# Output projection of the mixing stage as three products of high and low parts, W_out gated and split in pieces

## The chip, the core and the metric

One core of one Trainium2 chip runs the whole program. The metric is the device time of that core in microseconds, from the first to the last instruction with the launch's own overhead around it; the median of three runs counts.

## The reference

The block takes x (4 batches of 1024 tokens, 256 wide) and six modulation rows per batch, of which `ga` gates the mixing branch.

```
h = layernorm(x) * (1 + ca) + sa
xn = rms_scale * h / (norm(h) + 1e-8) * split_scale
K = sigmoid(xn @ W_K);  u, g_in, g_out = split(xn @ W_ugg, 3)
u = u * sigmoid(g_in) * (1 - K)
outputs = scan over time of (Kshift, u)
x = x + ga * (outputs * sigmoid(g_out) @ W_out + h)
h = layernorm(x) * (1 + cb) + sb
x = x + gb * mixture_of_experts(h)        # top 2 of 8, gelu, 256 -> 1024 -> 256
```

All of it is float32. What the change touches is the product `outputs * sigmoid(g_out) @ W_out`, with `ga` already multiplied into the columns of W_out.

## The kernel before

The program has two stages. The mixing stage (0 to about 287 us) handles 4096 tokens in 8 groups of 512 (`NG`), two groups to a batch; the expert stage, which this change leaves alone, handles sorted tiles of 256 tokens. Every engine has its program written out by hand, in order; semaphores connect them, and each engine runs strictly in its own order.

In a group g the hidden width of 512 is cut in four parts hc of 128. Where full precision is wanted, a float32 operand is rounded to a high part in a faster format (fp32r), the low part is what the rounding left out, and a product is taken as high*high + high*low + low*high. The kernel before does that for the main products, not for the output projection.

TensorE, `main(g, hc)`: 24 products of 512 columns into the four banks mm[0] to mm[3] (K, g_in, u, g_out), in two halves `main_part`. `project(g, hc)`, L814: four float32 products of 256 columns, `og` with `wog`, each recorded as two passes. Between them the turns `turn_xn` (L804) and `turn_h2` (L832), `logits` and `rank`. The order in a group is main_part(0), turn_h2(g-2), main_part, project(g-1, 3), logits(g-2), main(g,1), project(g,0), rank(g-2), main(g,2), project(g,1), main_part(g,3,0), turn_xn(g+1), main_part(g,3,1), project(g,2).

ScalarE, `gates_in` and `gate_out`: the sigmoids of K into `kb` (L643), of g_in into `sgi` (L646), of g_out in place (L651). Between them the scalings and squares of the two norms (`sqj`, `sqk`, L612, L621, L628, L659, L668), the high part `xh` of the turned input (L635), the copies of turned h2 (L675) and the gate sigmoid `sgw` (L680).

VectorE, `recur(g, hc)`: four steps of 128x512, L1046 (u times g_in, releases `u_gated`), L1049, the scan L1052 and the output gate `og` (L1057), double-buffered; for even g a copy of the scan's last column, `cy`. Between the four calls stand the small chains of the norms (`ln1_stats`, `ln1_norm`, `ln2_stats`), the choice of experts (`top2`, `place`, `gate_weights`), `xn_low` (L1039) and `add_y` (L1070, L1075), which takes the finished projection out of PSUM. A function `weave` issues one step of each of several chains in turn, since each step of a chain waits for the one before it.

GpSimd: `ln1_modulate`, `ln2_modulate` and `gate_h`, two 128x1024 operations each (L471 and L474, L497 and L500, L490 and L491), paced by `u_gated` through `beside`; `gate_wout(b)` (L480), one operation of 128x1024 per batch that makes `wog`, double-buffered; and `send`, four indirect DMA issues at a time (L510) that put rows of h2 in their experts' lists.

Around the change the order of GpSimd and ScalarE counts most. GpSimd's loop before:

```
for g in range(NG):
    if g == 0:
        gate_wout(0)
        ln1_modulate(1)
    beside(g, 0)
    gate_h(g)
...
    if g % 2 == 1 and g + 1 < NG:
        gate_wout(g // 2 + 1)
...
    if g >= 2:
        send(g - 2, 0)
```

## Time and profile before

| | |
|---|---|
| median of 3 runs | 784.33 us (784.13 to 784.36) |
| the profiled execution | 783.47 us, its span 781.5 us |
| mean granted TensorE clock | 0.956 |
| TensorE busy | 707.0 us, 90% of the span |
| VectorE busy | 534.0 us, 68% |
| ScalarE busy | 421.0 us, 54% |
| GpSimd busy | 399.8 us, 51% |
| chain that ended last | TensorE 70%, VectorE 12%, issue 8% |
| of it the output projection, L814 | 6% |

PE stands for TensorE's products, PEld for its weight loads, DVE for VectorE, ACT for ScalarE, POOL for GpSimd. Busy time is the time in which an engine has at least one operation under way; an operation that stands still on the engine counts as busy. The mixing stage is the first 287 of the 781.5 us.

### The profile page before, as it was taken

The page shows a single profiled execution, that of the slowest core. Times are in us where ns is not written, and L with a number is a line of the kernel's source. Part 1 is how long each engine was busy: PE and PEld are TensorE (multiplying, and loading weights), DVE is VectorE, ACT ScalarE, POOL GpSimd, SP SyncE. Part 2 cuts the span into 40 slices and gives each one's busy share as a digit, 9 for nine tenths or more (in the row PEclk, how much of TensorE's full clock was granted, in tenths as well). Part 3 has the DMA queues.
Part 4 walks back from the last instruction along what each step waited for, and adds up shares of the span by engine and source line. Part 5 has one row for each costly group of instructions (what it writes and reads, how often), then busy time and mean ns, then how long its engine had stood idle before and what let it go on. Part 6 is the DMA issues. An engine that isn't in the chain of part 4 may idle for free.

```text
span 781.5 us, 17355 instructions
## 1 busy us (share of the span) xinstructions
PE 707.0 (90%) x4854; PEld 652.7 (84%) x4854; DVE 534.0 (68%) x1787; ACT 421.0 (54%) x1082; POOL 399.8 (51%) x309
## 2 busy tenths in 40 slices
PE   4899999999999964699998999989889989999992
PEld 1778888888888853699998999989879989989991
DVE  6878879989796768375557655576684576485551
ACT  6466555655545342356656556656446565565560
POOL 1355647777583465445436435454554363463443
PEclk9899999999999995699999999999898999999997
DMA  8531012130120522534364343747423644433432
GB/s 298 163 137 55 3 54 97 54 110 29 55 76 22 177 83 77 184 57 68 65 145 96 63 75 62 175 110 179 109 46 61 138 105 109 81 54 66 68 70 41
DMA packets 50309, 72.56 MB, mean 93 GB/s; under 512 B 5808, under 2 KB 42108, under 8 KB 50240
## 3 DMA queue, kind: packets, MB, share of 16 engines
q0 software_dynamic: 16480, 27.28, 19.3%
q1 hardware_dynamic: 33760, 44.46, 18.1%
q8 instruction: 30, 0.49, 0.3%
q14 instruction: 39, 0.32, 0.1%
HBM read 48.85 MB, written 22.87 MB: 92 GB/s over the span
## 4 chain that ended last, share of the span: by engine, by line
PE 70%; DVE 12%; issue 8%; ACT 3%; DMA 3%; another core or an unknown queue 1%; POOL 1%; DVEq 0%; POOLq 0%; ACTq 0%
PE mm L945 21%; PE mm L789 19%; PE yb L955 18%; PE yb L814 6%; PE tp L924 2%; DMA out_x<-ysb,tokb 1%; DVE hl L1307 1%; DVE SL L238 1%; PE tp L845 1%; DMA gbr<-mod_rows,xm 1%; PE tp L804 1%; PE tp L832 1%; DVE fl L1271 1%; DVE SH L230 1%
## 5 line engine op out<-in xcount | busy, mean ns | idle before, releaser
L763 ACT ACTIVATE h<-mm,b1T 128x256 f32<-128x256 f32 (+1 forms) x288 | 134.4, 467 | 187.9 <-PE mm L945 116.0
L1307 DVE TENSOR_TENSOR hl<-h,hh 128x256 fp32r<-128x256 f32 (+1 forms) x288 | 121.0, 424 | 139.7 <-ACT hh L764 107.5
L555 POOL DMA_INDIRECT out_x<-ysb,tokb x68 | 112.5, 1654 | 202.2 <-DVE ysb L1338 170.3
L945 PE MATMUL mm<-fh,SH 128*128 128x256 f32 x576 | 166.3, 289 | 21.0 <-DVE fl L1271 13.8
L955 PE MATMUL yb<-SH,hh 128*128 128x256 f32 x544 | 157.9, 290 | 9.7 <-DVE hl L1307 9.4
L945 PE MATMUL mm<-fl,SH 128*128 128x256 f32 x576 | 164.8, 286 | 0.0
L945 PE MATMUL mm<-fh,SL 128*128 128x256 f32 x576 | 164.5, 286 | 0.0
L955 PE MATMUL yb<-SH,hl 128*128 128x256 f32 x544 | 153.6, 282 | 0.0
L955 PE MATMUL yb<-SL,hh 128*128 128x256 f32 x544 | 153.3, 282 | 0.0
L764 ACT ACTIVATE hh<-mm,b1T 128x256 fp32r<-128x256 f32 (+1 forms) x288 | 133.7, 464 | 0.0
L945 PEld LDWEIGHTS mm<-fh,SH 128*128 128x128 f32 x576 | 112.6, 195 | 23.6 <-issue 23.6
L955 PEld LDWEIGHTS yb<-SH,hh 128*128 128x128 f32 x544 | 103.2, 190 | 12.2 <-DVE hl L1307 11.1
L945 PEld LDWEIGHTS mm<-fl,SH 128*128 128x128 f32 x576 | 112.3, 195 | 0.0
L945 PEld LDWEIGHTS mm<-fh,SL 128*128 128x128 f32 x576 | 112.3, 195 | 0.0
L789 PE MATMUL mm<-xh,WH 128*128 128x512 f32 x256 | 107.0, 418 | 1.5 <-DVE xl L1039 1.4
L955 PEld LDWEIGHTS yb<-SL,hh 128*128 128x128 f32 x544 | 103.4, 190 | 0.0
L955 PEld LDWEIGHTS yb<-SH,hl 128*128 128x128 f32 x544 | 103.2, 190 | 0.0
L789 PE MATMUL mm<-xh,WL 128*128 128x512 f32 x256 | 101.2, 395 | 0.0
L789 PE MATMUL mm<-xl,WH 128*128 128x512 f32 x256 | 100.5, 393 | 0.0
L550 POOL DMA_INDIRECT gbr<-mod_rows,xm x74 | 75.7, 1022 | 22.6 <-issue 22.6
L510 POOL DMA_INDIRECT disp_x<-h2all,pos x64 | 63.6, 994 | 28.9 <-issue 26.2
L814 PE MATMUL yb<-wog,og 128*128 128x256 f32 x256 | 60.3, 379 | 0.0
(217 smaller groups left out, 1182.7 us busy)
## 6 DMA issues: line engine op xcount, KB each, us to landing
...
gbr<-mod_rows,xm POOLq DMA_INDIRECT x74
```

What stands on the lines that cost most here:

```text
L230: e.tensor_copy(SH[n % 2][:, r], wraw[n % 2][:, r]).then_inc(done, 1)
L510: e.indirect_dma_start(out=Xd, out_offset=bass.IndirectOffsetOnAxis(ap=p[:, j:j + 1], axis=0), in_=h2all[:, j, :], in_offset=None).then_in ...
L550: e.indirect_dma_start(out=gbr[:, j, :], out_offset=None, in_=modd.rearrange("b (n d) -> (b n) d", d=D), in_offset=bass.IndirectOffsetOnAx ...
L555: e.indirect_dma_start(out=out_rows, out_offset=bass.IndirectOffsetOnAxis(ap=tokb[:, j:j + 1], axis=0), in_=ysb[:, j, :], in_offset=None, ...
L763: e.activation(h32[:, f % 2, c_], mm[f % 4][:, c_], ACT.Gelu_apprx_tanh, bias=bias)
L764: e.activation(hh[:, f, c_], mm[f % 4][:, c_], ACT.Gelu_apprx_tanh, bias=bias)\
L789: i = e.matmul(mm[q][:, :], a[:, k, c0:c0 + 128], b[:, g % 2, k, :], start=(k == 0 and t == 0), stop=(k == 1 and t == 2))
L814: i = e.matmul(yb[j // 2][:, (j % 2) * D:(j % 2 + 1) * D], og[:, n % 2, j * 128:(j + 1) * 128], wog[:, (g // 2) % 2, hc, :], start=(hc == ...
L924: i = e.transpose(tp[k][:, j * 128:(j + 1) * 128], xin[:, j, k * 128:(k + 1) * 128], ident[:, :])
L945: i = e.matmul(mm[f % 4][:, 0:TE], a[:, k, f * 128:(f + 1) * 128], b[:, k, :], start=(k == 0 and t == 0), stop=(k == 1 and t == 2))
L955: i = e.matmul(yb[0][:, j * D:(j + 1) * D], a[:, f, j * 128:(j + 1) * 128], b[:, f, :], start=(f == 0 and j == 0 and t == 0), stop=(f == N ...
L1307: e.tensor_tensor(hl[:, f, w_], h32[:, f % 2, w_], hh[:, f, w_].bitcast(F32), ALU.subtract)\
```

## The change

Each call of `project` takes three fp32r products for every float32 product before: `oh` with `wgh`, `oh` with `wgl`, `ol` with `wgh`. For that, `og` (now one buffer) is copied by ScalarE to its high part `oh` (`o_high`), and VectorE subtracts (`o_low`) to get `ol`; `project` waits for `o_low`. `o_high(n-1)` stands in `gates_in` of the next part, between `kb` and `sgi`. `o_low` stands alone after `add_y` (hc 0) and after `recur(g, 2)`, and is woven into the chains that follow for hc 1 (after four steps) and hc 3 (after three).

W_out times `ga` is made in four pieces of 128x256 per batch. GpSimd multiplies a piece into `wgt` (two buffers, `gate_wout(b, h)`), ScalarE copies it to `wgh` (`wout_high`), GpSimd subtracts it to `wgl` (`wout_low`). `wgh` and `wgl` have one buffer, so a piece of the next batch waits for the last `project` that reads it. The pieces are issued at the start of the first group of a batch, ahead of `gate_h`, not at the end of the group before it. For the first batch `modulate(1)` on VectorE replaces `ln1_modulate(1)` on GpSimd. To make room, `sqk` is gone (its operation shares `sqj`), and two small buffers of the start lie in others.

The core of the diff (the new semaphores `wout_high`, `wout_low`, `o_high`, `o_low` and the small buffers are left out):

```diff
...
             ob = sb(p1, "ob", [128, T])
-            og = sb(p1, "og", [128, 2, T])
-            wog = sb(p1, "wog", [128, 2, 4, D])
+            og = sb(p1, "og", [128, T])
+            oh = sb(p1, "oh", [128, 2, T], F32R)
+            ol = sb(p1, "ol", [128, 2, T], F32R)
+            wgh = sb(p1, "wgh", [128, 4, D], F32R)
+            wgl = sb(p1, "wgl", [128, 4, D], F32R)
+            wgt = sb(p1, "wgt", [128, 2, D])
...
             sqj = sb(p1, "sqj", [128, 4, D])
-            sqk = sb(p1, "sqk", [128, 4, D])
...
-            def gate_wout(b):
+            def gate_wout(b, h):
...
                 e.wait_ge(S[f"mod_loaded{b % 3}"], 16 * (b // 3 + 1))
-                past(e, "projected", 8 * (b - 1))
-                e.tensor_tensor(wog[:, b % 2, :, :], wo[:, :, :], bc(mod(b, 2), 4), ALU.mult)\
-                    .then_inc(S["wout_gated"], 1)
+                past(e, "wout_low", 4 * b + h - 1)
+                e.tensor_tensor(wgt[:, h % 2, :], wo[:, h, :], mod(b, 2), ALU.mult).then_inc(S["wout_gated"], 1)
+            def wout_low(b, h):
+                e.wait_ge(S["wout_high"], 4 * b + h + 1)
+                e.tensor_tensor(wgl[:, h, :], wgt[:, h % 2, :], wgh[:, h, :].bitcast(F32), ALU.subtract)\
+                    .then_inc(S["wout_low"], 1)
...
             for g in range(NG):
-                if g == 0:
-                    gate_wout(0)
-                    ln1_modulate(1)
+                if g % 2 == 0:
+                    gate_wout(g // 2, 0)
+                    gate_wout(g // 2, 1)
+                    wout_low(g // 2, 0)
+                    gate_wout(g // 2, 2)
+                    wout_low(g // 2, 1)
+                    if g == 0:
+                        gate_wout(0, 3)
+                    wout_low(g // 2, 2)
+                    if g == 0:
+                        wout_low(0, 3)
...
                 gate_h(g)
+                if g and g % 2 == 0:
+                    gate_wout(g // 2, 3)
...
                     ln1_modulate(g + 2)
+                if g and g % 2 == 0:
+                    wout_low(g // 2, 3)
...
                     ln2_modulate(g - 1)
-                if g % 2 == 1 and g + 1 < NG:
-                    gate_wout(g // 2 + 1)
...
                 past(e, "h_squared", g)
+                past(e, "x2_squared", g - 2)
...
                     e.activation(xh[:, g % 2, k, :], tp[k][:, :], ACT.Copy).then_inc(S["xn_high"], 1)
+            def wout_high(b, h):
+                e.wait_ge(S["wout_gated"], 4 * b + h + 1)
+                past(e, "projected", 4 * (2 * b - 1) + h + 1)
+                e.activation(wgh[:, h, :], wgt[:, h % 2, :], ACT.Copy).then_inc(S["wout_high"], 1)
+            def o_high(n):
+                e.wait_ge(S["o_gated"], n + 1)
+                past(e, "projected", n - 1)
+                e.activation(oh[:, n % 2, :], og[:, :], ACT.Copy).then_inc(S["o_high"], 1)
...
                 e.activation(kb[:, hc, 1:T + 1], mm[0][:, :], ACT.Sigmoid).then_inc(S["k_ready"], 1)
+                if n:
+                    o_high(n - 1)
...
                 past(e, "x2_squared", g)
+                e.wait_ge(S["h_squared"], min(g + 3, NG))
                 for j in range(4):
-                    i = e.activation(sqk[:, j, :], x2b[:, g % 2, j, :], ACT.Square, bias=sm2[:, 1, j:j + 1],
+                    i = e.activation(sqj[:, j, :], x2b[:, g % 2, j, :], ACT.Square, bias=sm2[:, 1, j:j + 1],
...
             for g in range(NG):
+                if g and g % 2 == 0:
+                    for h in range(3):
+                        wout_high(g // 2, h)
...
                 gate_out(g, 0)
+                if g and g % 2 == 0:
+                    wout_high(g // 2, 3)
...
                 gates_in(g, 1)
+                if g == 0:
+                    for h in range(4):
+                        wout_high(0, h)
...
             g = NG - 1
+            o_high(4 * NG - 1)
...
                 n = 4 * g + hc
-                e.wait_ge(S["o_gated"], n + 1)
-                e.wait_ge(S["wout_gated"], g // 2 + 1)
+                e.wait_ge(S["o_low"], n + 1)
+                e.wait_ge(S["wout_low"], 4 * (g // 2) + hc + 1)
...
                 for j in range(4):
-                    i = e.matmul(yb[j // 2][:, (j % 2) * D:(j % 2 + 1) * D], og[:, n % 2, j * 128:(j + 1) * 128],
-                                 wog[:, (g // 2) % 2, hc, :], start=(hc == 0 and j % 2 == 0), stop=(hc == 3),
-                                 skip_group_check=True)
+                    for t, (a, b) in enumerate(((oh, wgh), (oh, wgl), (ol, wgh))):
+                        i = e.matmul(yb[j // 2][:, (j % 2) * D:(j % 2 + 1) * D], a[:, n % 2, j * 128:(j + 1) * 128],
+                                     b[:, hc, :], start=(hc == 0 and j % 2 == 0 and t == 0), stop=(hc == 3 and t == 2),
+                                     skip_group_check=True)
...
+            def modulate(g):
+                e.wait_ge(S["x_scaled"], g + 1)
+                link(e, e.tensor_tensor(hb[:, g, :, :], hb[:, g, :, :], bc(mod(0, 1), 4), ALU.mult), "dve_a")
+                e.tensor_tensor(hb[:, g, :, :], hb[:, g, :, :], bc(mod(0, 0), 4), ALU.add).then_inc(S["h_ready"], 1)
...
                 e.wait_ge(S["out_gated"], n + 1)
-                past(e, "projected", n - 1)
-                e.tensor_tensor(og[:, n % 2, :], ob[:, :], mm[3][:, :], ALU.mult).then_inc(S["o_gated"], 1)
+                past(e, "o_high", n)
+                past(e, "o_low", n)
+                e.tensor_tensor(og[:, :], ob[:, :], mm[3][:, :], ALU.mult).then_inc(S["o_gated"], 1)
...
                     link(e, e.tensor_copy(cy[:, hc:hc + 1], ob[:, T - 1:T]), "dve_a")
+            def o_low(n, rounds):
+                for _ in range(rounds):
+                    yield
+                e.wait_ge(S["o_high"], n + 1)
+                past(e, "projected", n - 1)
+                e.tensor_tensor(ol[:, n % 2, :], og[:, :], oh[:, n % 2, :].bitcast(F32), ALU.subtract)\
+                    .then_inc(S["o_low"], 1)
...
             e.wait_ge(S["mod0_copied"], 2)
-            e.wait_ge(S["x_scaled"], 1)
-            link(e, e.tensor_tensor(hb[:, 0, :, :], hb[:, 0, :, :], bc(mod(0, 1), 4), ALU.mult), "dve_a")
-            e.tensor_tensor(hb[:, 0, :, :], hb[:, 0, :, :], bc(mod(0, 0), 4), ALU.add).then_inc(S["h_ready"], 1)
+            modulate(0)
...
             for g in range(NG):
+                n = 4 * g
+                low = [o_low(n - 1, 3)] if g >= 1 else []
...
                 elif g + 2 < NG:
-                    weave(ln1_stats(g + 2), ln1_norm(g + 1))
+                    weave(ln1_stats(g + 2), ln1_norm(g + 1), *low)
                 elif g + 1 < NG:
-                    weave(ln1_norm(g + 1))
+                    weave(ln1_norm(g + 1), *low)
+                else:
+                    weave(*low)
...
                     add_y(g - 1)
+                else:
+                    modulate(1)
+                weave(o_low(n, 0))
...
                 if g == 0:
-                    weave(ln1_norm(1), ln1_stats(2))
-                weave(*([ln2_stats(g - 1)] if g >= 1 else []), *([place(g - 2), gate_weights(g - 2)] if g >= 2 else []))
+                    weave(ln1_norm(1), ln1_stats(2), o_low(n + 1, 4))
+                else:
+                    weave(ln2_stats(g - 1), *([place(g - 2), gate_weights(g - 2)] if g >= 2 else []), o_low(n + 1, 4))
...
                 recur(g, 2)
+                weave(o_low(n + 2, 0))
...
                 recur(g, 3)
+            weave(o_low(4 * NG - 1, 0))
...
```

The order on GpSimd from the end of group 3 to the start of group 4. In it `disp_x<-h2all` is `send`, `wog` and `wgt` are W_out times `ga`, `wgl` its low part. Before:

```order
L497 TENSOR_TENSOR h2all<-h2all,mb 128x4x256 [waits s_x2_scaled]
L500 TENSOR_TENSOR h2all<-h2all,mb 128x4x256 [waits s_u_gated,s_pool_own]
L480 TENSOR_TENSOR wog<-wo,mb 128x1024 [waits s_projected,s_mod_loaded2,s_wout_loaded]
L510 DMA disp_x<-h2all,pos 34816x264 [waits s_pads_sent0,s_pads_zeroed,s_weights_ready,s_places_ready]
L510 DMA disp_x<-h2all,pos 34816x264 x3
```

With the change:

```order
L507 TENSOR_TENSOR h2all<-h2all,mb 128x4x256 [waits s_u_gated,s_pool_own]
L517 DMA disp_x<-h2all,pos 34816x264 [waits s_pads_sent0,s_pads_zeroed,s_weights_ready,s_places_ready]
L517 DMA disp_x<-h2all,pos 34816x264 x3
L483 TENSOR_TENSOR wgt<-wo,mb 128x256 [waits s_wout_low,s_mod_loaded2,s_wout_loaded] x2
L487 TENSOR_TENSOR wgl<-wgt,wgh 128x256 [waits s_wout_high]
L483 TENSOR_TENSOR wgt<-wo,mb 128x256 [waits s_wout_low,s_mod_loaded2,s_wout_loaded]
L487 TENSOR_TENSOR wgl<-wgt,wgh 128x256 [waits s_wout_high] x2
L497 TENSOR_TENSOR hb<-hb,mb 128x1024 [waits s_xn_ready,s_x_loaded1,s_mod_loaded2,s_u_gated]
```

The operation on W_out stood ahead of the sends; its pieces now stand behind them.

The order on ScalarE at the same place, from the squares that end group 3 (`sqj`) to the sigmoids of part 0 of group 4. Before:

```order
L621 ACTIVATE sqj,ss<-hb 128x256 x3
L641 ACTIVATE kb<-zcol 128x1 [waits s_k_ready,s_scanned]
L643 ACTIVATE kb<-mm 128x512 [waits s_main_done,s_act_own]
L646 ACTIVATE sgi<-mm 128x512 [waits s_u_gated,s_main_done]
L675 ACTIVATE h2T<-tp 128x512 [waits s_h2_turned,s_logits_done]
```

With the change:

```order
L640 ACTIVATE sqj,ss<-hb 128x256 x3
L659 ACTIVATE wgh<-wgt 128x256 [waits s_projected,s_wout_gated] x3
L670 ACTIVATE kb<-zcol 128x1 [waits s_k_ready,s_scanned]
L672 ACTIVATE kb<-mm 128x512 [waits s_main_done,s_act_own]
L664 ACTIVATE oh<-og 128x512 [waits s_projected,s_o_gated]
L677 ACTIVATE sgi<-mm 128x512 [waits s_u_gated,s_main_done]
L707 ACTIVATE h2T<-tp 128x512 [waits s_h2_turned,s_logits_done]
```

Three copies `wgh` now stand ahead of `kb`, and wait for GpSimd (`wout_gated`); `oh` stands between `kb` and `sgi`.

The order on VectorE at `recur(3, 2)` and behind it. Before:

```order
L1046 TENSOR_TENSOR mm<-mm,sgi 128x512 [waits s_main_done,s_in_gated]
L1049 SCALAR_TENSOR_TENSOR mm<-kb,mm 128x512 [waits s_u_gated,s_k_ready]
L1052 SCALAR_TENSOR_TENSOR ob<-kb,cy,mm 128x512 [waits s_w_ready]
L1057 TENSOR_TENSOR og<-ob,mm 128x512 [waits s_projected,s_out_gated,s_scanned]
L1039 TENSOR_TENSOR xl<-tp,xh 128x512 [waits s_xn_high] x2
L1046 TENSOR_TENSOR mm<-mm,sgi 128x512 [waits s_main_done,s_in_gated]
```

With the change:

```order
L1093 TENSOR_TENSOR mm<-mm,sgi 128x512 [waits s_main_done,s_in_gated]
L1096 SCALAR_TENSOR_TENSOR mm<-kb,mm 128x512 [waits s_u_gated,s_k_ready]
L1099 SCALAR_TENSOR_TENSOR ob<-kb,cy,mm 128x512 [waits s_w_ready]
L1105 TENSOR_TENSOR og<-ob,mm 128x512 [waits s_o_high,s_o_low,s_out_gated,s_scanned]
L1115 TENSOR_TENSOR ol<-og,oh 128x512 [waits s_projected,s_o_high]
L1086 TENSOR_TENSOR xl<-tp,xh 128x512 [waits s_xn_high] x2
L1093 TENSOR_TENSOR mm<-mm,sgi 128x512 [waits s_main_done,s_in_gated]
```

`ol` stands between the output gate and `xl`, and waits for ScalarE's `o_high`.

## Rows read from the trace of the kernel before

**Rows 1.** windows, columns us, then busy (x) of PE, PEld, DVE, ACT, POOL

```profile
134.40:167.14 32.74, 32.23 (x163) 26.86 (x162) 30.79 (x115) 18.01 (x48) 25.74 (x17) 1.00 0.23 76
```

**Rows 2.** chain that ended last: start us, us, what

```profile
167.14 1.73 PE yb L814 x8
168.98 5.61 PE mm L789 x24
...
344.50 1.42 PE yb L955 x12
```

**Rows 3.** waits of DVE, 134.4 to 167.1 us: total, times, longest

```profile
DVE xl L1039 <- ACT xh L635: 0.4, 1, 0.4
```

**Rows 4.** timeline of DVE: start us, us, engine line op

```profile
110.61 0.70 DVE L1046 TENSOR_TENSOR mm<-mm,sgi 128x512 f32<-128x512 f32 x1
...
131.37 2.16 DVE L1104 TENSOR_TENSOR rt<-Lg,mx 128x32 f32<-128x32 f32 x1
...
143.85 0.70 DVE L1046 TENSOR_TENSOR mm<-mm,sgi 128x512 f32<-128x512 f32 x1
...
148.99 0.69 DVE L1046 TENSOR_TENSOR mm<-mm,sgi 128x512 f32<-128x512 f32 x1
...
151.83 0.69 DVE L1057 TENSOR_TENSOR og<-ob,mm 128x512 f32<-128x512 f32 x1
152.43 1.40 DVE L989 BATCH_NORM_STATS2 bst<-xb 128x6 f32<-128x256 f32 x4
153.75 0.84 DVE L1008 TENSOR_SCALAR nt<-ss 128x4 f32<-128x4 f32 x1
...
157.72 0.68 DVE L1046 TENSOR_TENSOR mm<-mm,sgi 128x512 f32<-128x512 f32 x1
...
162.77 1.68 DVE L1075 TENSOR_SCALAR sm<-sm 128x4 f32<-128x4 f32 x1
...
167.38 0.69 DVE L1046 TENSOR_TENSOR mm<-mm,sgi 128x512 f32<-128x512 f32 x1
...
172.71 0.18 DVE L1126 TENSOR_SCALAR exw<-sgw 128x36 f32<-128x36 f32 x1 [0.72 <-ACT sgw L680]
...
175.64 0.70 DVE L1046 TENSOR_TENSOR mm<-mm,sgi 128x512 f32<-128x512 f32 x1
...
241.09 0.70 DVE L1046 TENSOR_TENSOR mm<-mm,sgi 128x512 f32<-128x512 f32 x1
```

**Rows 5.** timeline of ACT

```profile
147.14 1.10 ACT L635 ACTIVATE xh<-tp 128x512 fp32r<-128x512 f32 x2
...
150.52 0.41 ACT L621 ACTIVATE sqj<-hb 128x256 f32<-128x256 f32 x1
...
153.20 0.60 ACT L643 ACTIVATE kb<-mm 128x512 f32<-128x512 f32 x1 [0.89 <-PE mm L789]
...
171.47 0.60 ACT L643 ACTIVATE kb<-mm 128x512 f32<-128x512 f32 x1
```

**Rows 6.** timeline of POOL

```profile
147.05 2.43 POOL L497 TENSOR_TENSOR h2all<-h2all,mb 128x1024 f32<-128x1024 f32 x1
149.82 2.37 POOL L500 TENSOR_TENSOR h2all<-h2all,mb 128x1024 f32<-128x1024 f32 x1 [0.34 <-DVE mm L1046]
...
154.71 0.99 POOL L510 DMA_INDIRECT disp_x<-h2all,pos  x1 [0.15 <-issue]
...
159.55 2.38 POOL L490 TENSOR_TENSOR hb<-hb,mb 128x1024 f32<-128x1024 f32 x1
```

**Rows 7.** line L238, duration ns min/median/max

```profile
L238 DVE TENSOR_TENSOR SL<-h2all,SH x20: 678/684/5294, 328.3 to 693.8; 128x512 fp32r<-128x512 f32 x20
```

**Rows 8.** timeline of PE, idle before in brackets

```profile
49.44 1.10 PE L804 MATMUL tp<-ident,xnb 128*128 128x128 f32 x8 [1.37 <-ACT xnb L628]
```

**Rows 9.** PE at 553.5, and the window behind it (PEclk after the engines)

```profile
553.50 0.58 PE L955 MATMUL yb<-SH,hh 128*128 128x256 f32 x1 [3.69 <-DVE hl L1307]
...
553.40:560.00 6.60, 6.50 (x32) 6.50 (x33) 4.20 (x13) 2.44 (x6) 1.87 (x2) 0.54 0.55 173
```

More of the change, by code:

```diff
@@ L35 @@
     "c_silu", "scale_made", "mod_made", "mod0_copied", "mod_copied", "mod_guarded", "mod_written", "mod_loaded0",
-    "mod_loaded1", "mod_loaded2", "zero_made", "pads_zeroed", "w_high", "w_low", "wout_gated", "b1_copied",
+    "mod_loaded1", "mod_loaded2", "zero_made", "pads_zeroed", "w_high", "w_low", "wout_gated", "wout_high", "wout_low", "o_high", "o_low", "b1_copied",
     "x_stats", "x_scaled", "h_ready", "h_squared", "rms_ready", "xn_ready", "xn_turned", "xn_high", "xn_low",
@@ L71, in build @@
         zcol = sb(ctx, "zcol", [128, 1])
-        vrow = sb(ctx, "vrow", [76, 128])
         vT = sb(ctx, "vT", [128, 76])
@@ L78, in build @@
         bgb = sb(ctx, "bgb", [128, E])
-        ioi = sb(ctx, "ioi", [128, 210], I32)
         iof = sb(ctx, "iof", [128, 210])
@@ L163, in build @@
         modr = x2f[0:NB, 0:6 * D]
+        ioi = x2f[:, 0:210].bitcast(I32)
+        vrow = h2T[0:76, 0, 0:128]
         mtmp = x2f[0:NB, 6 * D:8 * D].rearrange("p (a d) -> p a d", a=2)
@@ L605, in mod_rows @@
                 e.wait_ge(S["mod_made"], n + 3)
+                e.wait_ge(S["iota_made"], 7 + E // 2)
                 e.activation(modr[:, n * 512:(n + 1) * 512], mm[n][0:NB, :], ACT.Copy).then_inc(S["mod_copied"], 1)
```

## The prediction

> **What bounds the kernel now.** I read the page first: TensorE is busy 90% of the span and holds 70% of the chain that ended last. Then the windows, for the mixing stage, the only one that the change touches: in one group period of 32.7 us TensorE is busy 32.2, VectorE 30.8, GpSimd 25.7, ScalarE 18.0 [rows 1]. The chain gives TensorE's pieces: one `project` takes 1.73 us, one `main` 5.6 [rows 2]. So TensorE paces the stage, and VectorE is close behind; that is the second thing to see. Third, VectorE's list of waits: in that period it waited 0.4 us in all [rows 3]. The other periods leave it up to 4 us, but here it has no room, against the 1.2 us that TensorE can give back per group.
>
> I write R0(g) to R3(g) for the start of VectorE's `recur(g, h)`, its first row L1046. R2 is at 110.61, 143.85, 175.64 and 241.09 for g = 2, 3, 4, 6 [rows 4]: 130.5 us for the four cycles from R2(2) to R2(6).
>
> **The change, part by part.**
> *TensorE.* Each of 32 calls of `project` becomes 12 products of 256 columns. The expert stage has that shape, 12 of them in 1.42 us [rows 2]. So 32 x (1.73 - 1.42) = 9.9 us less, 1.24 per group. If TensorE went on pacing, that would be the result.
>
> *VectorE and ScalarE.* 32 subtractions `o_low` of 128x512. The nearest row is `og`, 0.69 us long, 0.60 to the next start [rows 4]: 2.4 us per group, twice what TensorE gives. 32 copies `o_high`, 0.6 long and 0.5 from start to start as `xh` (two in 1.10) [rows 5]: no load at ScalarE's 18 us, but each stands in line between `kb` and `sgi` and waits for `og`. `og` loses its second buffer; since `o_low(n)` always stands ahead of the next use on VectorE, this costs nothing of its own. The price falls in four legs of VectorE's cycle.
>
> *Leg R2 to R3*, 5.1 us before (143.85 to 148.99). `og(g,2)` ends 3.5 after R2 (151.83 + 0.69 against 148.99, the same four steps [rows 4]). ScalarE then copies, so `o_low` could start at 4.25. But GpSimd's L497 runs from 3.2 to 5.6 us after R2 [rows 6], and operations with both operands in SBUF stand still under such a piece: L1104, 32 numbers wide, took 2.16 us, and L1075, four wide, 1.68 [rows 4]. `o_low` reads `og` and `oh`, both in SBUF; of the 128x512 subtractions of that kind in the expert stage one took 5.29 us where the median is 0.68 [rows 7]. So it starts at 5.65, 0.6 later `xl` (1.2) follows: the leg becomes 7.45.
> The Trainium skill, SBUF — State Buffer, section "SBUF: two separate sides", says why: the port pair that VectorE and GpSimd share is an exclusive lock, kept for a whole instruction, which a VectorE operation with two SBUF inputs takes as well. By that rule the hold is certain, and where VectorE is first, GpSimd is held instead.
> Without any hold the leg would be 6.4 (it still waits for `oh`, then `xh`), and the sum 4.2 us less; that is the lower bound.
>
> *Leg R3 to R0 of the next group*, 8.7 before (148.99 to 157.72), of which 0.7 was L1008 held under GpSimd's old L480. Now 8.0 plus 0.6 for the woven `o_low`: 8.6 (8.8 for even g, with the copy of `cy`; 1.8 less from g = 5 on, where no `ln1_stats` is left).
> At a change of batch the largest term comes in. GpSimd issues the first `gate_wout` behind `send(g-2, 0)`, where L480 stood ahead of it, and ScalarE has three `wout_high` ahead of `gates_in(g, 0)`: both excerpts of the order show it. GpSimd ended L500 3.2 us after R3 (149.82 + 2.37 against 148.99); four sends take 4.85 (154.71 to 159.55) [rows 6]. Then come wgt, wgt, wgl, wgt, with ScalarE's copies between: a 128x1024 piece takes 2.4 [rows 6], a quarter some 0.65, the ScalarE copy 0.4 (L621, 128x256) [rows 5]. So the third copy ends at R3 + 3.2 + 4.85 + 2.6 + 0.45 = R3 + 11.1. Before, `kb(4, 0)` ran at R3 + 4.2 (153.20) [rows 5]. Now `kb`, `oh` and `o_low(3, 3)` start at 11.1, 11.6 and 12.3, where the weave would issue `o_low` at 5.8. VectorE stands 6.5 us behind it, and TensorE some 5 us ahead of `project(3, 3)`. The same at g = 6 (6.1); at g = 2 no sends lie in the way and it is 1.3. Bounds: nothing, if GpSimd were ahead, against which speaks that L500 waits for VectorE's own `u_gated(g, 3)`; and 8, if each small piece costs 1 us.
>
> *Leg R0 to R1*, 9.7 before (157.72 to 167.38), 1.6 of it the hold of L1075. With `gate_h` on time its two pieces of 2.4 end 5.65 us after R0, then `o_low` 0.6 and `top2` 3.0 (164.4 to 167.38): 9.3. For g = 3, where the pad writes make GpSimd late, I add one more piece of hold, 2.3: 11.6.
>
> *Leg R1 to R2*, 7.9 and 8.3 before. Where VectorE is late, `og` ends at 3.5, `oh` starts at 3.6, `sgi` and the gate's sigmoid follow 0.5 apart, VectorE's L1126 has it at 4.85, and from L1126 to the next `recur` it is 2.93 (172.71 to 175.64), now plus 0.6: 8.4. Where VectorE isn't late, the end T of `main(g,1)` on TensorE sets it: `kb` at T + 4.5 (171.47 against 167.0), `oh` at T + 5.0, R2 = T + 9.8; `o_low(g,1)` then ends at T + 8.3, where TensorE is ready for `project(g,1)` at T + 7.1, and waits 1.2 us, as much as the four calls of the group give.
>
> **Sum.** Cycle from g = 2: 7.45 + 8.8 + 11.6 + 8.4 = 36.3; from 3: 7.45 + 8.6 + 6.5 + 9.3 + 8.4 = 40.2; from 4: 7.45 + 8.8 + 9.3 + 8.4 = 34.0; from 5: 7.45 + 6.8 + 6.1 + 9.3 + 8.4 = 38.0. Together 148.5 against 130.5: + 18.0. Ahead of R2(2), TensorE gains 2.5 on eight calls and the 1.4 us wait for `xnb(1)` [rows 8], since `modulate(1)` moves from GpSimd to VectorE; against it stand three waits of 1 to 1.8 us for the first `wgl` and `ol`, the 1.3 at g = 2 and 1.2 at `project(2,1)`: + 1.5 in VectorE's R2. From R2(6) to R2(7) TensorE and the T rule give 32.6 as before. In the tail two calls of `project` are 0.6 shorter in all: - 0.5. The expert stage has the same instructions. The merged buffers (`sqj`, `x2b`) wait for steps long done: nothing. Sum + 19. The profiled execution took 783.47 (span 781.5), so 802.5; the median shown, 784.33, lies 0.9 above it: **803 us**.
>
> **The rivals.**
> (1) TensorE goes on pacing: 784.3 - 9.9 = 774.4, the other side. For it: TensorE has no gap now, and the woven `o_low` falls into chains of small steps with gaps between them. Against it: the 0.4 us of waits [rows 3] and ScalarE's order. It decides if the sends cost GpSimd under 1 us ahead of `wgt` instead of 4.85, and `o_low(g,1)` ends 1.2 us earlier than I work out. Chance 0.09.
> (2) Only the waits that hang on one engine's order come true: TensorE's two stalls of 5.2, and 1.2 for six `project(g,1)`; VectorE hides the rest. 784.3 - 9.9 + 10.4 + 7.2 = 792, from 786 to 795. For it: my legs add every hold in full, and holds move as GpSimd's times do. Chance 0.18.
> (3) The stalls also cost TensorE its clock. After an idle stretch of 3.7 us ahead of 553.50 the granted clock was 0.54 over 6.6 us, nearly its lower level, 1.2 GHz [rows 9]. A stall of 5 us at g = 4 and 6 could do the same, 3.3 us each. VectorE is 3 us behind TensorE there, so most of it hides; if not, 803 + 6.6 = 810, and with longer holds up to 816. Chance 0.1.
> (4) The 12 products take as long as the 8 passes did: that changes only rival 1, since in the forecast TensorE waits anyway.
> The forecast itself, 796 to 809 (four holds of 1.05 and 2.5 of the waits down; two longer stalls of 1.5 and more holds up): chance 0.63.
>
> **How the numbers follow.** The range reaches over rival 2 and most of rival 3 and leaves out rival 1: 786 to 814. A measurement of this kernel can tell about 0.2%, 1.6 us, from no change. Faster: rival 1 and a little of rival 2's low end, 0.1. Same: rival 2's low end, 0.03. Slower: 0.87.
>
> **What would show it.** Right: in the mixing stage TensorE waits ahead of its `yb` products for VectorE's `ol`, 1 to 2 us in a group and about 5 us twice; ScalarE's `wgh` rows stand idle behind GpSimd's sends; some `ol` rows last 1.5 to 3 us instead of 0.69; the stage ends near 305 us instead of 286, and from there both traces run alike. Wrong: TensorE stays without a gap (rival 1), or VectorE's rows show waits for TensorE in every group (rival 2). The weakest step is the batch change: if `wgh` is not late, 12.6 of my 19 us are gone.

## The result, and the profile after

The changed kernel takes 830.06 us (median of 4 runs, 828.86 to 831.18) against 784.35 of the kernel before on the same chip: ratio 1.0574, 95% interval 1.0553 to 1.0595. The forecast of 803 us, 786 to 814, had the direction, but the loss is 45.7 us where it said 19.

The profiled execution took 831.01 us, its span 829.2. The page first: TensorE is busy 87% of it for 90 before, and its busy time has grown, 720.2 us for 707.0, though the products of the change need less of it. The second row shown gives the clock that it was granted, in tenths of full speed, in 40 slices of 20.7 us; the 9th (166 to 187) and the 13th (249 to 269 us), both 7, hold two stalls that this text comes to.

```profile
PE 720.2 (87%) x4982; PEld 662.7 (80%) x4982; DVE 563.1 (68%) x1821; ACT 443.9 (54%) x1130; POOL 411.9 (50%) x335
...
PEclk9799989979997999568999999999988999999997
```

Where before one period of the mixing stage had no room on TensorE and 0.4 us of waits on VectorE [rows 1, 3], now the period from R2(3) to R2(4), 159.66 to 204.47, is 44.8 us long and nobody fills it (columns as in [rows 1], then the granted clock):

```profile
159.66:204.47 44.81, 36.47 (x183) 30.87 (x182) 30.41 (x115) 22.23 (x57) 27.20 (x21) 0.85 0.14 48
```

VectorE's waits in it, and the longest of ScalarE's (total, times, longest):

```profile
DVE ol L1115 <- ACT oh L664: 12.1, 3, 7.0
```

```profile
ACT wgh L659 <- POOL wgt L483: 16.0, 4, 7.5
```

VectorE stands 12.1 us ahead of `ol` for ScalarE's `oh`; ScalarE stands 16.0 us ahead of `wgh` for GpSimd's `wgt`. The timeline gives the legs: `recur` begins with L1093 now (L1046 in [rows 4]).

```profile
122.00 0.70 DVE L1093 TENSOR_TENSOR mm<-mm,sgi 128x512 f32<-128x512 f32 x1
...
159.66 0.70 DVE L1093 TENSOR_TENSOR mm<-mm,sgi 128x512 f32<-128x512 f32 x1
...
166.94 0.68 DVE L1093 TENSOR_TENSOR mm<-mm,sgi 128x512 f32<-128x512 f32 x1
...
179.87 0.69 DVE L1115 TENSOR_TENSOR ol<-og,oh 128x512 fp32r<-128x512 f32 x1 [7.03 <-ACT oh L664]
...
182.63 0.70 DVE L1093 TENSOR_TENSOR mm<-mm,sgi 128x512 f32<-128x512 f32 x1
...
192.58 0.69 DVE L1115 TENSOR_TENSOR ol<-og,oh 128x512 fp32r<-128x512 f32 x1 [4.36 <-ACT oh L664]
...
196.16 0.69 DVE L1093 TENSOR_TENSOR mm<-mm,sgi 128x512 f32<-128x512 f32 x1
...
204.47 0.70 DVE L1093 TENSOR_TENSOR mm<-mm,sgi 128x512 f32<-128x512 f32 x1
...
284.11 0.70 DVE L1093 TENSOR_TENSOR mm<-mm,sgi 128x512 f32<-128x512 f32 x1
```

R2(2) is at 122.00 for 110.61, R2(3) to R2(4) is 44.8 for 31.8, R2(2) to R2(6) is 162.1 for 130.5. Leg R3(3) to R0(4) is 15.7 us long with 7.03 of idle ahead of `ol`; the leg R0(4) to R1(4) is 13.5 with 4.36 of idle ahead of the next `ol`. The chain of waits through both (start us, us, what):

```profile
174.18 0.96 POOL disp_x L517
175.17 1.41 POOL wgt L483 x2
176.58 0.69 POOL wgl L487
177.43 0.73 POOL wgt L483
...
178.50 0.20 ACT kb L670
...
179.22 0.63 ACT oh L664
179.87 0.69 DVE ol L1115
...
182.63 0.71 DVE mm L1093
183.41 2.35 POOL hb L497
...
188.16 0.74 POOL wgt L483
...
189.25 0.32 ACT hb L630
...
189.74 1.57 ACT hb L630 x3
...
191.93 0.63 ACT oh L664
192.58 0.69 DVE ol L1115
```

The first stall is the one that was forecast: `send`, then `wgt`, `wgl`, `wgt`, then `kb`, `oh`, `ol`. The second was not: `gate_h` (hb L497, and L498 behind it), the fourth `wgt` at 188.16, ScalarE's fourth `wgh`, its four scalings `hb` (L630), and only then `kb(4,1)`, `oh(4,0)` and `ol(4,0)`.

Behind the stage 5 us more are lost: from R3(7) to the end it is 507.6 us (829.2 - 321.59) for 502.8 (781.5 - 278.73). In the chain 3 us of them are one piece, ahead of `Lg`, whose releaser the profile does not name; before (first) and after:

```profile
288.30 1.42 another core or an unknown queue
```

```profile
331.06 4.45 another core or an unknown queue
```

Most versions below have 3.3 to 4.5 us in that place, with and without the splits; e13 and e14 have none. What VectorE waits for there stays open. It isn't all: in the ten versions below with 4.4 to 4.5 us there, the time from R3(7) to the end still runs from 502.2 (e11) to 508.6 us (e5). That part has nothing to do with the change as far as I can see, so I give the length of the stage beside the ratios.

### The profile page after: what moved, and what is told of

Same layout as the page of the kernel before. It is cut to its first block, busy times and chain, and to the rows that moved or that the text cites. A ratio compares the mean times of both kernels' runs of the same rounds, so it can differ in the third digit from the quotient of the medians.

```text
span 829.2 us, 17844 instructions
## 1 busy us (share of the span) xinstructions
PE 720.2 (87%) x4982; PEld 662.7 (80%) x4982; DVE 563.1 (68%) x1821; ACT 443.9 (54%) x1130; POOL 411.9 (50%) x335
## 4 chain that ended last, share of the span: by engine, by line
PE 51%; DVE 23%; issue 11%; ACT 6%; POOL 5%; another core or an unknown queue 2%; DMA 1%; DVEq 0%; SPq 0%; ACTq 0%; POOLq 0%
PE mm L987 21%; PE yb L997 19%; PE mm L830 5%; DVE ol L1115 3%; DVE ob L1099 2%; PE tp L966 2%; PE yb L856 2%; DVE mm L1093 2%; DVE hl L1372 1%; DVE mm L1096 1%; POOL wgt L483 1%; DVE SL L241 1%; POOL disp_x L517 1%; DVE xl L1086 1%
## 5 line engine op out<-in xcount | busy, mean ns | idle before, releaser
L1372 DVE TENSOR_TENSOR hl<-h,hh 128x256 fp32r<-128x256 f32 (+1 forms) x288 | 123.4, 430 | 142.9 <-ACT hh L805 124.5
L987 PE MATMUL mm<-fh,SH 128*128 128x256 f32 x576 | 166.3, 289 | 22.1 <-DVE fl L1336 12.1
L987 PEld LDWEIGHTS mm<-fh,SH 128*128 128x128 f32 x576 | 112.3, 195 | 24.7 <-issue 14.5
L997 PEld LDWEIGHTS yb<-SH,hh 128*128 128x128 f32 x544 | 103.7, 191 | 12.8 <-DVE hl L1372 11.7
L830 PE MATMUL mm<-xh,WL 128*128 128x512 f32 x256 | 104.4, 408 | 0.0
L830 PE MATMUL mm<-xl,WH 128*128 128x512 f32 x256 | 104.0, 406 | 0.0
L856 PE MATMUL yb<-wgh,oh 128*128 128x256 f32 x128 | 39.7, 310 | 26.5 <-DVE ol L1115 26.4
```

Of the source, the lines that this page charges most:

```text
L830: i = e.matmul(mm[q][:, :], a[:, k, c0:c0 + 128], b[:, g % 2, k, :], start=(k == 0 and t == 0), stop=(k == 1 and t == 2))
L856: i = e.matmul(yb[j // 2][:, (j % 2) * D:(j % 2 + 1) * D], a[:, n % 2, j * 128:(j + 1) * 128], b[:, hc, :], start=(hc == 0 and j % 2 == 0 ...
L987: i = e.matmul(mm[f % 4][:, 0:TE], a[:, k, f * 128:(f + 1) * 128], b[:, k, :], start=(k == 0 and t == 0), stop=(k == 1 and t == 2))
L997: i = e.matmul(yb[0][:, j * D:(j + 1) * D], a[:, f, j * 128:(j + 1) * 128], b[:, f, :], start=(f == 0 and j == 0 and t == 0), stop=(f == N ...
L1372: e.tensor_tensor(hl[:, f, w_], h32[:, f % 2, w_], hh[:, f, w_].bitcast(F32), ALU.subtract)\
```

## The experiments

**Theory A**: the loss is made at the changes of batch, where ScalarE stands behind GpSimd's pieces, with the split of o on top. **Rivals**: the products, or a lower clock that comes with them, cost the time (B); VectorE's own added work does (C); GpSimd's late pieces do, whatever ScalarE's order (D). The kernel before was timed again beside each set of runs, with medians of 782 to 786 us, so I compare ratios to it; 0.01 of ratio is 7.84 us. "Stage" is the start of `recur(7,3)` in the trace, R3(7): 278.73 before, 321.59 after.

**Both splits off (e1).** VectorE writes `og` rounded, GpSimd `wog`; `project` takes `enumerate(((og, wog), (og, wog), (og, wog)))`; both low parts are left out. The diffs of this section show the lines that carry each edit; `...` stands for others.

```diff
-                e.tensor_tensor(og[:, :], ob[:, :], mm[3][:, :], ALU.mult).then_inc(S["o_gated"], 1)
+                e.scalar_tensor_tensor(og[:, n % 2, :], ob[:, :], 1.0 / 3, mm[3][:, :], ALU.mult, ALU.mult)\
+                    .then_inc(S["o_gated"], 1)
...
+                e.tensor_tensor(wog[:, b % 2, :, :], wo[:, :, :], bc(mod(b, 2), 4), ALU.mult)\
```

> The changed kernel without both splits: VectorE writes ob times the gate straight into a rounded og (two buffers again, times 1/3, so that three equal products og x wog sum to about the same output), GpSimd gates W_out in one 128x1024 operation into a rounded wog, as before the change; the low parts of the output projection are left out. TensorE keeps its three products a slice. Theory A (VectorE's waits for ScalarE and GpSimd at the batch changes, with the split of o on top, make the loss): 772 to 778 us, since what is left of the change is the 12 products in 1.42 us for four in 1.73. Rival B (the products themselves, or TensorE's clock, cost the time): 795 us or more.

Measured: 779.99 us, ratio 0.9935 (0.9914 to 0.9956), stage 274.2. That is 2 us above what A gave, and far below B: the products cost nothing, they give back 5.1 us, 4.6 by the stage. (This run has no stalls either, so it says nothing of what the clock costs behind a stall; see e9.) In the chain that ended last, all of it TensorE's from 140 to 180 us, a `project` lasts 1.43 (before 1.73 [rows 2]):

```profile
160.70 5.61 PE mm L790 x24
166.31 1.43 PE yb L816 x12
```

**o unsplit, W_out still in pieces (e2).** `og` has two rounded buffers, `oh` and `ol` are gone, and with them the low part of o.

```diff
-                    for t, (a, b) in enumerate(((oh, wgh), (oh, wgl), (ol, wgh))):
+                    for t, (a, b) in enumerate(((og, wgh), (og, wgl), (og, wgl))):
```

> The changed kernel with W_out still split in pieces, but og written rounded by VectorE with no high copy on ScalarE and no subtraction on VectorE (the low part of o is left out; the third product takes wgl again). Theory A: ScalarE still stands ahead of kb(g,0) and of kb(g,1) until GpSimd has gated its pieces, so the batch changes keep most of their 11.4 and 13.1 us of stall: 800 to 812 us. Rival C (VectorE's own added work, 32 subtractions and their handshakes, is the loss): 775 to 785 us.

797.83 us, ratio 1.0152 (1.0115 to 1.0189), stage 291.4; somewhat below what A gave and far above C.

**W_out unsplit, o still split (e3).** `gate_wout(b)` is one operation at the end of the odd group again; the low part of W_out is left out.

```diff
-                    for t, (a, b) in enumerate(((oh, wgh), (oh, wgl), (ol, wgh))):
+                    for t, (a, b) in enumerate(((oh, wog), (ol, wog), (ol, wog))):
```

> The changed kernel with o still split, but W_out gated in one 128x1024 operation at the end of the odd group into a rounded wog, two buffers, as before the change (the low part of W_out is left out; the third product takes ol again). Theory A: the stalls at the three batch changes go: about 30 us less than the changed kernel, 796 to 804 us. Rival C: 820 to 830 us.

802.74 us, ratio 1.0214 (1.0183 to 1.0246), stage 295.7, as A gave. With the changed kernel the three make a square: from e1, W_out's split alone costs 0.0217 (17.0 us), o's alone 0.0279 (21.9 us), both 0.0639 (50.1 us), so 11 us come only where both meet. I read them as ScalarE's stall, which then holds up `oh`, and VectorE with it, besides `kb`; e11 below bears that out. C, which forecast 775 to 785 and 820 to 830 for the last two, fails as the only cause; but o's split by itself is as large as W_out's.

**ScalarE's order mended (e4).**

```diff
             for g in range(NG):
-                if g and g % 2 == 0:
-                    for h in range(3):
-                        wout_high(g // 2, h)
                 gates_in(g, 0)
...
                 gate_out(g, 0)
                 if g and g % 2 == 0:
-                    wout_high(g // 2, 3)
+                    for h in range(3):
+                        wout_high(g // 2, h)
...
                 gate_out(g, 1)
+                if g and g % 2 == 0:
+                    wout_high(g // 2, 3)
```

> The changed kernel with one thing moved: ScalarE takes the first three wout_high of a batch behind gate_out(g,0) and the fourth behind gate_out(g,1), so that neither kb(g,0) nor kb(g,1) and the high copies of o behind them stand behind a wait for GpSimd. All arithmetic as in the changed kernel. Theory A: ScalarE's place is what stalls, about 7 us at R3 to R0 and 4.4 us at R0 to R1 of each batch change: 800 to 808 us. Rival D (GpSimd's late pieces hold the projection itself, whatever ScalarE's order): 825 to 832 us, with the wait moved to project's wait for wgl.

809.9 us, ratio 1.0312 (1.0285 to 1.0339), stage 301.7: 20.5 us less than the change by moving four instructions, 2 us short of what A gave. D fails. The granted clock of the profiled execution rose from 0.929 to 0.951.

**Only the fourth (e9), and only the first three (e10) of these moves.** e9 has the last two hunks' moves of `wout_high(g // 2, 3)` alone; in e10 all four stand in the place where the fourth stood:

```diff
                 gate_out(g, 0)
                 if g and g % 2 == 0:
-                    wout_high(g // 2, 3)
+                    for h in range(4):
+                        wout_high(g // 2, h)
```

> The changed kernel with the fourth wout_high alone moved behind gate_out(g,1); the first three still stand ahead of kb(g,0). Theory A: ol(g,0) waits no longer for ScalarE at R0 to R1 (4.36 us idle at 192.58 and 4.37 at 108.56 in the changed kernel, three batch changes), the 7 us at R3 to R0 stay: 816 to 822 us. Rival: the two stalls have one cause (GpSimd is late) and the time only moves: 827 us or more.

> The changed kernel with the first three wout_high moved behind gate_out(g,0), where the fourth stands already; the fourth still stands ahead of ln1_scale and kb(g,1). Theory A: the waits of ol for ScalarE at R3 to R0 (7.03 us at 179.87, 8.72 at 259.40) go for the most part, those at R0 to R1 stay: 812 to 818 us. Rival: as for e9, 827 us or more, or all of e4's gain, 808 to 811 us, if the fourth cost nothing by itself.

821.87 and 818.62 us, ratios 1.0486 (1.0451 to 1.0522) and 1.0424 (1.0393 to 1.0455): 6.9 and 11.8 us less than the change. Together 18.7, near e4's 20.5: two stalls with a price each, as A says; e10 came out 0.6 us above its range. In e10 the leg R3(5) to R0(6) falls from 15.6 to 7.1, and the fourth `wout_high` then eats some of it: R0(6) to R1(6) grows from 11.8 to 16.4.

In e9 the leg R0 to R1 falls from 13.6 to 9.3 at g = 2, but only from 13.5 to 11.7 at g = 4, and stays at 11.8 at g = 6. There the first stall is still in place, and TensorE's clock is low behind it: TensorE stood 6.5 us before 175.67 and before 254.04, and then got half of its clock, 1.2 GHz (windows of e9, columns as above):

```profile
175.66:184.50 8.84, 8.83 (x35) 8.25 (x36) 7.38 (x36) 3.35 (x8) 5.81 (x4) 0.50 0.02 1
254.00:262.70 8.70, 8.66 (x34) 8.12 (x35) 6.96 (x25) 1.32 (x4) 5.73 (x4) 0.50 0.09 30
```

ScalarE's `kb(4,1)` and `kb(6,1)` wait for TensorE's products, and `ol` behind them:

```profile
184.67 0.60 ACT L672 ACTIVATE kb<-mm 128x512 f32<-128x512 f32 x1 [4.80 <-PE mm L830]
263.04 0.60 ACT L672 ACTIVATE kb<-mm 128x512 f32<-128x512 f32 x1 [7.72 <-PE mm L830]
264.19 0.69 DVE L1115 TENSOR_TENSOR ol<-og,oh 128x512 fp32r<-128x512 f32 x1 [2.64 <-issue]
```

VectorE stands 2.5 us there at g = 4 (ahead of 185.82) and 2.6 at g = 6 (the profile says `issue`, but ScalarE's `oh` ended just before, at 264.16). At these two changes of batch the fourth copy and the low clock lie side by side, and to take away the copy alone gives back little.

**ScalarE's order mended, o unsplit (e11).** The diffs of e2 and e4 together.

> e2_o_unsplit (W_out in pieces, og written rounded by VectorE, the low part of o left out) with ScalarE's order of e4_scalar_late. Theory A: of e2's 17.8 us above e1, nearly all is ScalarE's place: 782 to 787 us. Rival G (GpSimd's 24 more operations and what they hold of VectorE are the larger part): 790 to 798 us.

785.18 us, ratio 1.0017 (0.9996 to 1.0037), stage 280.6, as A gave. Of W_out's 17.0 us, 10.6 were ScalarE's place; 6.4 are left. With o split the same place is worth 20.5 (e4), so nearly all of the 11 us that need both splits belong to it.

The 6.4 us lie in the leg R0 to R1 at the changes of batch: 12.34, 11.04 and 12.37 in e11 for 8.54, 9.64 and 10.04 in e1, while the legs R3 to R0 ahead of them are about the same in sum. The pieces put GpSimd's `gate_h` later, beside the choice of experts (`top2`), whose small operations then take 2 us for 0.19. GpSimd first (L496, as long, follows at 98.93), then VectorE, in e11:

```profile
96.45 2.40 POOL L495 TENSOR_TENSOR hb<-hb,mb 128x1024 f32<-128x1024 f32 x1
```

```profile
96.87 2.04 DVE L1146 TENSOR_TENSOR rt<-Lg,mx 128x32 f32<-128x32 f32 x1
99.38 2.06 DVE L1149 TENSOR_TENSOR sel<-iof,rmin 128x32 f32<-128x32 f32 x1
```

The small pieces hold VectorE too, as the timelines of e4 show, GpSimd first, then VectorE:

```profile
170.36 1.42 POOL L483 TENSOR_TENSOR wgt<-wo,mb 128x256 f32<-128x256 f32 x2
171.73 0.74 POOL L487 TENSOR_TENSOR wgl<-wgt,wgh 128x256 fp32r<-128x256 f32 x1
```

```profile
169.61 0.16 DVE L1027 SCALAR_TENSOR_TENSOR nt<-nt 128x4 f32<-128x4 f32 x1
169.73 0.75 DVE L1026 SCALAR_TENSOR_TENSOR nt<-nt 128x4 f32<-128x4 f32 x1
170.41 0.75 DVE L1052 TENSOR_TENSOR nt<-nt 128x4 f32<-128x4 f32 x1
171.08 1.42 DVE L1027 SCALAR_TENSOR_TENSOR rsn<-nt,rsn 128x4 f32<-128x4 f32 x1
172.42 0.15 DVE L1053 TENSOR_SCALAR nt<-nt 128x4 f32<-128x4 f32 x1
```

Three steps that are 0.1 us apart elsewhere take 2.7 there. The first stands beside the end of a `send` (to 170.34); the next two end within 0.1 us of a piece of GpSimd (171.07 and 172.47).

**Is o's split dear because `ol` is held?** In e4 `ol(4,2)` lasts 2.61 us. e5 puts `xn_low(g + 1)` ahead of `o_low(n + 2, 0)`; e7 also leaves `og` in PSUM:

```profile
196.01 2.61 DVE L1115 TENSOR_TENSOR ol<-og,oh 128x512 fp32r<-128x512 f32 x1 [0.69 <-DVE cy L1107]
198.54 1.27 DVE L1086 TENSOR_TENSOR xl<-tp,xh 128x512 fp32r<-128x512 f32 x2
```

```diff
-                weave(o_low(n + 2, 0))
                 if g + 1 < NG:
                     xn_low(g + 1)
+                weave(o_low(n + 2, 0))
```

> e4_scalar_late with one thing moved on VectorE: at hc=2 the two subtractions xl(g+1) stand ahead of the subtraction ol(g,2). In e4 ol(g,2) begins beside GpSimd's 128x1024 product of ln2_modulate and takes 2.61 us for 0.69 (196.01), while xl(g+1), which reads PSUM, takes 0.64 each after it. Theory E (the subtraction is held until GpSimd's operation ends, and what reads PSUM is not held): the leg R2 to R3 falls from about 7.9 to about 7.0 us at seven groups, so 802 to 806 us against 809.9. Rival F (the row is long because of something else, or the hold moves on to xl or to the next operation): legs unchanged, 808 to 812 us.

```diff
-KINDS = (("k_ready", 0), ("in_gated", 2), ("scanned", 1), ("o_gated", 3))
+KINDS = (("k_ready", 0), ("in_gated", 2), ("scanned", 1), ("o_low", 3))
...
-                e.tensor_tensor(ol[:, n % 2, :], og[:, :], oh[:, n % 2, :].bitcast(F32), ALU.subtract)\
+                e.tensor_tensor(ol[:, n % 2, :], mm[3][:, :], oh[:, n % 2, :].bitcast(F32), ALU.subtract)\
```

> e5 with og left in PSUM: VectorE writes ob times the gate back into the gate's bank, ScalarE makes the high copy from there, and the subtraction ol reads it there; the bank is free for TensorE only when ol is done, not when og is. Theory E: no ol row is longer than 0.75 us (in the changed kernel the 32 rows sum to 32.3 us, 10.2 above 32 x 0.69), and 2 to 6 us less than e5. Rival I (TensorE waits for the bank instead): waits of main for ol appear, and the time is 3 us or more above e5.

e5: 809.94 us, ratio 1.0271 (1.0208 to 1.0333), too wide to tell from e4's; its stage, 301.7, is e4's. By the time it is rival F that holds, though the row did what E says, and the leg fell from 7.97 to 7.02 at g = 4, 2.9 us over g = 1 to 5. But the same leg grew by 1.9 at g = 0 and 6 together, where VectorE waited longer for `xh` than it had been held, and R0(2) to R1(2) by 0.5. At g = 4:

```profile
198.00 1.29 DVE L1086 TENSOR_TENSOR xl<-tp,xh 128x512 fp32r<-128x512 f32 x2 [1.68 <-ACT xh L654]
199.20 0.68 DVE L1115 TENSOR_TENSOR ol<-og,oh 128x512 fp32r<-128x512 f32 x1
```

e7: 815.33 us, ratio 1.039 (1.033 to 1.045), stage 309.9. The line of `ol` (ns, min/median/max), and what TensorE waits for between 28 and 330 us:

```profile
L1114 DVE TENSOR_TENSOR ol<-mm,oh x32: 676/684/693, 36.5 to 314.1; 128x512 fp32r<-128x512 f32 x32
```

```profile
PE mm L829 <- DVE ol L1114: 26.6, 17, 3.0
```

No row is held any more, and it is no use: TensorE waits 26.6 us for the bank. Rival I was right. By the Trainium skill, SBUF — State Buffer, section "SBUF: two separate sides", an operation of VectorE takes the lock that it shares with GpSimd if both of its inputs are in SBUF, or if it runs in a 2-port mode. The trace agrees for the subtraction: with one input in PSUM 32 rows between 676 and 693 ns, where in e4 the longest was 2608.

**GpSimd's pieces elsewhere (e6, e8).** e6 is e5 with this; e8 is e7 with one `gate_wout` of 128x1024 in that place, and one high copy and one low part for three slices, the latter behind `beside(g, 0)`.

```diff
+                if g % 2 == 1 and g + 1 < NG:
+                    gate_wout(g // 2 + 1, 0)
+                    gate_wout(g // 2 + 1, 1)
                 if g >= 2:
                     send(g - 2, 0)
```

> e5 with one thing moved on GpSimd: the first two gated pieces of W_out of the next batch stand ahead of send(g-2,0) at the end of the odd group, not behind its four DMA issues (5.2 us). Theory G (with ScalarE's order mended, GpSimd's late pieces cost only by holding VectorE's small operations, three of which take 0.75, 0.75 and 1.42 us beside them at 169.73 in e4): the hold moves with the pieces and about the same is held: within 3 us of e5. Rival H (the projection's waits for its pieces still cost): 5 us or more less than e5.

> e7 with W_out gated in one 128x1024 operation ahead of send at the end of the odd group (the buffer of two pieces grows to four in the space that og left), the high copy of three slices in one activation and their low part in one operation that stands behind GpSimd's wait for the recurrence, so that it runs beside operations of VectorE that read PSUM. Theory G (what is left of W_out's split is hold of VectorE's small operations and ScalarE's place): 4 to 8 us less than e7, about 792 to 798 us. Rival J (what is left is GpSimd's added queue, and its later gate_h and ln1_modulate come late): same as e7 or above.

807.46 and 815.44 us, ratios 1.0273 (1.0224 to 1.0321) and 1.0363 (1.0315 to 1.041), stages 301.0 and 308.7: neither differs from its base by more than the intervals allow. e6 is as G says; e8 was forecast 4 to 8 us below e7 and isn't, so there rival J holds. Where GpSimd makes the pieces matters little once ScalarE doesn't wait for them.

**What of o's split costs?** On the kernel with W_out unsplit (e3): the subtraction made of 128 of its 512 columns (e12); the copy kept and the subtraction gone, `project` taking `oh` three times (e13); the subtraction kept and the copy gone, VectorE writing `oh` rounded and subtracting it from itself (e14). All three leave out low parts. The diffs are of e12 and e14:

```diff
-                e.tensor_tensor(ol[:, n % 2, :], og[:, :], oh[:, n % 2, :].bitcast(F32), ALU.subtract)\
+                e.tensor_tensor(ol[:, n % 2, 0:128], og[:, 0:128], oh[:, n % 2, 0:128].bitcast(F32), ALU.subtract)\
```

```diff
-                e.tensor_tensor(og[:, :], ob[:, :], mm[3][:, :], ALU.mult).then_inc(S["o_gated"], 1)
+                e.tensor_tensor(oh[:, n % 2, :], ob[:, :], mm[3][:, :], ALU.mult).then_inc(S["o_gated"], 1)
...
-                if n:
-                    o_high(n - 1)
...
-                e.wait_ge(S["o_high"], n + 1)
+                e.wait_ge(S["o_gated"], n + 1)
```

> e3_wout_unsplit with the subtraction ol made of 128 columns in place of 512 (the third product takes these for every slice, so the low parts of o are left out but for a quarter), everything else the same: the high copy, the waits, the products. Theory C' (what the split of o costs is VectorE's own time, 32 subtractions of 0.69 us): 786 to 792 us. Rival K (it is the way there and back over ScalarE, and the wait of the projection for it): 798 to 803 us.

> e3_wout_unsplit with ScalarE's high copy of o kept and VectorE's subtraction taken away: the projection waits for oh and takes it three times (og is scaled by 1/3); the low parts of the output projection are left out. Theory C' (VectorE's time is the price): 781 to 786 us, near e1's 780. Rival K (the way over ScalarE, one buffer of og): 792 us or more.

> e3_wout_unsplit with the subtraction kept at its places and its length (of oh and itself, so the low part of o is zero) and ScalarE's copy taken away: VectorE writes oh rounded itself, and the subtraction waits for nothing from another engine. Theory C': 796 to 802 us, near e3's 802.7. Rival K: 790 us or less.

| above both splits off (e1) | ratio to before | cost by it | stage | cost by it |
|---|---|---|---|---|
| copy alone, e13 | 0.9953 (0.9930 to 0.9976) | 1.4 us | 279.6 | 5.4 us |
| subtraction alone, e14 | 1.0149 (1.0114 to 1.0185) | 16.8 us | 291.0 | 16.9 us |
| both, a quarter of the subtraction, e12 | 1.0104 (1.0073 to 1.0135) | 13.3 us | 288.7 | 14.5 us |
| both, e3 | 1.0214 (1.0183 to 1.0246) | 21.9 us | 295.7 | 21.5 us |

The medians were 793.65 (e12), 778.66 (e13) and 791.67 us (e14). The totals of e13 and e14 are helped by the missing wait ahead of `Lg`; by the stage, copy and subtraction add up (5.4 + 16.9 for 21.5). C' is right in the main: the subtraction is three quarters of the price, though e12 and e14 came out between what the two theories said, and e13 below both. The way over ScalarE is the other quarter. A row that is shorter gives back less than its length: a quarter of the columns (0.293 us for 0.692, medians) gave back 7 to 9 us of 12.8 us of rows. The lines of `ol` in e3 and e12 (ns, min/median/max) show that the longest stays:

```profile
L1085 DVE TENSOR_TENSOR ol<-og,oh x32: 678/692/2833, 39.7 to 299.9; 128x512 fp32r<-128x512 f32 x32
```

```profile
L1086 DVE TENSOR_TENSOR ol<-og,oh x32: 277/293/2433, 40.2 to 292.9; 128x128 fp32r<-128x128 f32 x32
```

No version that keeps all of the arithmetic is faster than the kernel before; e1 and e13 are, without the low parts.

## Why the prediction failed

The path from before to after, in runs: products -5.1 us (e1); W_out's pieces with ScalarE in a good order +6.4 (e11); o's split on that +23.1 (e4); ScalarE's place +20.5; sum +45. By the stage the same steps are -4.6, +6.4, +21.1 and +19.9. Against the forecast, by legs of the profiled execution: the part ahead of R2(2) is 9.9 us longer, the four cycles from R2(2) to R2(6) 13.6 (legs R2 to R3 0.7, R3 to R0 3.7, R0 to R1 7.1, R1 to R2 2.2), the rest 5.2.

*The products*: 12 in 1.43 measured for 1.42, right. That the 9.9 us arrive only if TensorE paces is right too: with both splits off, half arrives. Rival 1 fell with VectorE's added work and ScalarE's order.

*Leg R2 to R3*, forecast 7.45: 7.93, 7.28, 7.97 and 7.27 for g = 2 to 5. The 6.4 that it gave without hold is borne out at g = 6, where `ol` took 0.98 us and the leg 6.35. In e13, without the subtraction, the leg is 6.42 too: it is the wait for `xh` that sets it. Right, with one loose reading: L1075 was taken for an operation with both inputs in SBUF, but it has one (`sm`), and such rows are held as well.

*Leg R3 to R0 at a change of batch*, forecast 15.1 at g = 4: 15.69. Right, to the order of GpSimd's rows. At g = 6, 12.9 forecast, 15.59 measured: the 1.8 us that I took off for the missing `ln1_stats` don't come off. `ol(5,3)` starts when ScalarE's queue lets it, 12.9 us after R3 at both changes of batch, so what VectorE saves ahead of it goes into the wait, 8.72 us for 7.03:

```profile
259.40 0.69 DVE L1115 TENSOR_TENSOR ol<-og,oh 128x512 fp32r<-128x512 f32 x1 [8.72 <-ACT oh L664]
```

(In e3, without that stall, the leg is 8.84, of which 2.0 is a hold: `ln1_norm`'s first step, four numbers, takes 2.17 us beside GpSimd's W_out operation.)

*Leg R0 to R1*, forecast 9.3: 9.17 at g = 5, but 13.61, 13.53 and 11.80 at g = 2, 4, 6 (the first lies ahead of R2(2)). **This is the first step that failed.** The prediction counts the three `wout_high` ahead of `gates_in(g, 0)` and never the fourth, ahead of `ln1_scale` and `gates_in(g, 1)`. It waits for a piece that GpSimd makes after two operations of 2.4 us that wait themselves for `recur(g, 0)`, and `kb(g,1)` and `oh(g,0)`, thus `ol(g,0)` and all of VectorE, stand behind it. Its undoing gives back 6.9 us (e9), most of it at g = 2; at g = 4 and 6 the leg stays at 11.7 and 11.8 for TensorE's low clock behind the first stall, and falls to 9.2 only if that went too (an estimate: e9's legs less the 2.5 and 2.6 us of waiting).

*The part ahead of R2(2)*, forecast +1.5: +11.4. **The second**, 9.9 us of the miss. I summed TensorE's waits there and took its gains against them, without walking VectorE's legs as in the later groups. In e1, R2(2) is at 110.41 for 110.61, so TensorE's gain of 3.9 us does not come; o's split takes it to 117.97 (e3), 0.76 us for each of ten subtractions; the pieces of W_out take it to 122.00, and the same fourth copy at g = 2 is enough to explain these 4.0 us: without it (e9) the leg R0 to R1 falls by 4.4.

*Sum of o's split*: outside the changes of batch the forecast has 19 - 13.9 = 5.1 us for it and the products together; e3 against before is 16.8.

*Leg R1 to R2*, forecast 8.4: 8.84, 8.31 and 8.37, but 10.24 at g = 6, where VectorE waits 1.4 and 1.5 us for ScalarE. I did not follow that further.

*Rival 3, the clock*: it fell as the rival said, and for 8.9 us (180.6 to 189.5) and 11.3 us (260.1 to 271.4) where it had 6.6. Behind the first stall (last columns: granted clock, DMA share, GB/s) TensorE ran at its lower level, 1.2 GHz:

```profile
186.60:189.30 2.70, 2.70 (x7) 2.14 (x8) 1.59 (x9) 0.38 (x2) 2.54 (x3) 0.50 0.00 1
```

But `kb(4,1)` began behind ScalarE's `hb`, at 191.43, when the six products for it were done at 189.5; there the fourth copy hid what the clock cost. At g = 6 the two end together: `kb(6,1)` runs at 269.15, 0.26 after ScalarE was free for it. So the rival's mechanism is right and its price came out small in this kernel only since a later stall covers it; with the fourth copy moved (e9) it is 2.5 and 2.6 us, and a part of what e4 and e10 gave back by removing the first stall is the clock's. How large a part, no run separates.

*The tail*, forecast -0.5: +4.8, of which 3.0 is the longer wait ahead of `Lg`. From R3(7) to VectorE's `x2b` it is 6.75 us for 6.84 before, so the copy and the subtraction ahead of the last `project` cost nothing; the other 1.9 us lie in the expert stage and stay open.
